# Fused LayerNorm, attention and mixture-of-experts on one core: the experts' code written out, their loop limits fetched early, and several pieces of work in a new order

## The chip, the cores and the metric

The kernel runs on one core of one Trainium2 chip. The metric is the device time of one execution in microseconds. A core has five engines with a sequencer each: TensorE (PE in the rows; its weight loads are PEld), VectorE (DVE), ScalarE (ACT), GpSimd (POOL) and SyncE (SP, which issues most DMAs). They work in parallel and meet only at semaphores.

## The reference

```python
xn = layernorm(x)                                   # x: 4 batches x 1024 rows x 256
q, k, v = xn @ Wq.T + bq, xn @ Wk.T + bk, xn @ Wv.T + bv
qk = einsum('bsd,btd->bst', q, k)
theta = 0.5 + 0.2 * sigmoid(qk) + 0.15 * tanh(qk) + 0.1 * relu(qk)
s = einsum('bst,btd->bsd', softmax(theta), v) @ Wo.T + bo
e = argmax(xn @ Wr + br)                            # one of 8 experts for each row
y = gelu(xn @ W1[e] + b1[e]) @ W2[e] + b2[e]        # hidden width 1024, exact gelu
out = x + s * silu(y)
```

## The kernel before

All products run on TensorE with operands split into a high and a low part. `product` (L812 to L815) makes three matmuls of one: high times high, high times low, low times high. So most operands are made in two steps: ScalarE or VectorE copies the high part (`high_...`), and VectorE subtracts it for the low part (`low_...`).

A tile is 128 rows of tokens; there are 32, eight to a batch. The order of the work is written out by hand on each engine, with semaphores in between. In order of time:

1. Batch 0. `scores(n)` makes the scores of tile n against its batch, `acts(n, h)` on ScalarE takes tanh and relu of each half, `thetas(n)` on VectorE mixes them and finds the greatest, `exps(n)` on ScalarE takes exp, `transposes(n)` on TensorE turns the result, `transposed_high` and `transposed_parts` split it, and `values(n)` multiplies it with v; `finish(n)` on VectorE scales the result. Between these, the other three batches are normalized (GpSimd, from `scales(3, ...)`), turned (`turn`, `keep_turned`), and their experts found (`route`, `take_turned`, `assign`). From the counts of tokens of each expert VectorE works out where each expert's units begin and end (`first_unit`, `last_unit`, `full_end`). The list of tokens sorted by expert is made with 32 small matmuls, `invert(t)`, eight of them behind the pieces of `values(5)`, 16 behind those of `values(6)`; they need `lanes` of VectorE and `token_at` of GpSimd.
2. The experts. A unit is 256 tokens of one expert, gathered by GpSimd. With the inputs of these runs there are 20, and the eight experts have 3, 1, 5, 1, 5, 1, 1 and 3 of them. TensorE does for each `hidden` (16 products, 48 matmuls), `turn_rows` of the next unit (4 transposes) and `expert_out` (8 products for each half of 128 tokens; where a unit holds at most 128, only one half). ScalarE does `gelus`, `row_high` and `gate`, VectorE `hidden_parts`, `row_low`, `biased` and `gated`. During the first unit of expert e the weights of e + 1 are split: `high_w1` and `high_w2` on ScalarE, `low_w1` and `low_w2` on VectorE, two pieces each. Experts 0 to 5 run in a loop over three pairs, with an inner loop over the units; 6 and 7 are written out. How far the inner loops run isn't known before the run: each engine reads `first_unit` and `full_end` into registers with `value_load` when it comes to an expert. Tiles 8 and 9 of batch 1 are scored between units of expert 7, and the rows of batch 2 are split by GpSimd (L492, L497).
3. Attention of batches 1 to 3, with the projections of the next batch (`job`) between.

An argument `head_slot` pads the code so that a loop's head stands at that slot of an instruction block.

## Time and profile before

| | |
|---|---|
| median of 3 runs | 550.07 us (549.77 to 550.94) |
| the profiled execution | 549.93 us, its span 548.1 us |
| TensorE busy in it | 526.6 us (96%) |
| VectorE, ScalarE, GpSimd busy | 413.5, 337.6, 206.3 us |
| the chain that ended last | TensorE 79%, VectorE 10%, ScalarE 5% |

TensorE sits idle for 21.5 us of the span. A matmul's end in the trace is modelled, so short pauses are seen in the distance from start to start rather than in the busy time. 1.8 us of the time lie outside the span.

### The profile page before, as it was taken

To read this page: it belongs to the slowest core of one execution; us is meant where nothing else is said; L and a number is where in the kernel's file an instruction comes from. 1 tells how busy PE (TensorE), PEld (TensorE's weight loads), DVE (VectorE), ACT (ScalarE), POOL (GpSimd) and SP (SyncE) were. 2 spreads that over 40 slices of the span, in tenths; PEclk is the share of its full clock that TensorE was granted. 3 is DMA by queue.
4 is the path that set the end of the run, shared out by engine and by line. 5 is a ranking of instruction groups with operands and counts; after the bars stand their busy time and mean duration, and the time that the engine had idled before them with its cause. 6 is when DMAs were issued, how large, how long until landed. Compare 5 with 4: busy or idle time off the path is not lost.

```text
span 548.1 us, 11163 instructions
## 1 busy us (share of the span) xinstructions
PE 526.6 (96%) x3891; PEld 496.4 (91%) x3892; DVE 413.5 (75%) x808; ACT 337.6 (62%) x607; POOL 206.3 (38%) x246
## 2 busy tenths in 40 slices
PE   7999999999999999999999989799999999999996
PEld 6888898998999999999999979798899899999995
DVE  6896688945588754787554897768899999777895
ACT  3587778536356733466433666278777877777881
POOL 2216338923112222122122214304467585333442
PEclk9999999999999999999999999999999999999999
DMA  8932920044315711146211411004132232111121
GB/s 285 333 153 107 337 78 1 1 139 160 125 59 150 245 45 50 46 148 226 85 38 52 130 50 39 19 21 155 59 108 95 88 115 88 59 42 46 59 67 49
DMA packets 40306, 56.88 MB, mean 104 GB/s; under 512 B 3607, under 2 KB 35358, under 8 KB 39726
## 3 DMA queue, kind: packets, MB, share of 16 engines
q1 hardware_dynamic: 35020, 45.62, 24.8%
q0 software_dynamic: 3488, 9.47, 6.0%
q10 hardware_dynamic: 1762, 1.32, 0.7%
q8 instruction: 20, 0.33, 0.2%
q14 instruction: 16, 0.13, 0.1%
HBM read 40.68 MB, written 17.56 MB: 106 GB/s over the span
## 4 chain that ended last, share of the span: by engine, by line
PE 79%; DVE 10%; ACT 5%; issue 4%; DMA 1%; DVEq 0%; ACTq 0%
PE ps L813 25%; PE ps L815 23%; PE ps L814 23%; PE ps L912 4%; PE ps L972 2%; PE ps L1085 1%; DVE stats L1220 1%; DVE theta L1278 1%; DVE theta L1274 1%; PE ps L962 1%; ACT theta L613 1%; ACT theta L603 1%; DMA xn_all<-in_L_attn_x_dram 1%; ACT tanh_s L604 1%; DVE u_lo L1255 0%
## 5 line engine op out<-in xcount | busy, mean ns | idle before, releaser
L712 ACT ACTIVATE hid<-ps,b_now 128x256 f32<-128x256 f32 x160 | 66.7, 471 | 42.3 <-PE ps L815 32.7
L813 PE MATMUL ps<-v_hi,pT_hi 128*128 128x258 f32 x256 | 76.2, 298 | 2.5 <-DVE pT_lo L1292 1.0
L814 PE MATMUL ps<-v_lo,pT_hi 128*128 128x258 f32 x256 | 72.5, 283 | 0.0
L815 PE MATMUL ps<-v_hi,pT_lo 128*128 128x258 f32 x256 | 72.3, 282 | 0.0
L1274 DVE SCALAR_TENSOR_TENSOR theta<-tanh_s,theta 128x512 f32<-128x512 f32 x64 | 49.1, 767 | 27.5 <-ACT tanh_s L604 26.8
L813 PE MATMUL ps<-rowT_h,w_hi_even 128*128 128x256 f32 x224 | 63.8, 285 | 1.1 <-issue 1.0
L815 PE MATMUL ps<-rowT_h,w_lo_even 128*128 128x256 f32 x224 | 63.5, 283 | 0.0
L814 PE MATMUL ps<-rowT_l,w_hi_even 128*128 128x256 f32 x224 | 63.4, 283 | 0.0
L483 POOL COPY unit_token<-sorted_token 128x2 int32 x19 | 4.6, 241 | 152.3 <-PE ps L1085 152.3
L613 ACT ACTIVATE theta<-theta,neg_max 128x512 f32<-128x512 f32 x64 | 42.9, 721 | 28.2 <-DVE neg_max L1278 27.9
L813 PE MATMUL ps<-w_hi_even,hidT_h 128*128 128x256 f32 x200 | 58.1, 291 | 0.2
L1546 DVE TENSOR_TENSOR hidT_l<-hid,hidT_h 128x512 fp32r<-128x512 f32 x80 | 55.4, 693 | 2.8
L815 PE MATMUL ps<-w_hi_even,hidT_l 128*128 128x256 f32 x200 | 56.6, 283 | 0.0
L814 PE MATMUL ps<-w_lo_even,hidT_h 128*128 128x256 f32 x200 | 56.6, 283 | 0.0
L720 ACT ACTIVATE g_sb<-y_sb 128x512 f32<-128x512 f32 x20 | 12.6, 632 | 70.1 <-DVE y_sb L1551 70.1
L603 ACT ACTIVATE theta<-ps,c_half 128x512 f32<-128x512 f32 x64 | 44.3, 692 | 18.6 <-PE ps L815 18.6
L813 PEld LDWEIGHTS ps<-v_hi,pT_hi 128*128 128x128 f32 x256 | 48.5, 189 | 3.7 <-issue 2.2
L813 PE MATMUL ps<-xnT_hi,u_hi 128*128 128x512 f32 x128 | 51.7, 404 | 0.0
L473 POOL DMA_INDIRECT row<-xn_rows,unit_token x38 | 43.6, 1147 | 20.7 <-POOL unit_token L483 14.9
L504 POOL DMA_INDIRECT g_tile<-sorted_g,slot_g x32 | 37.9, 1183 | 33.8 <-DMA sorted_g<-g_sb 28.4
L815 PE MATMUL ps<-xnT_hi,u_lo 128*128 128x512 f32 x128 | 50.2, 392 | 0.0
L814 PE MATMUL ps<-xnT_lo,u_hi 128*128 128x512 f32 x128 | 50.0, 391 | 0.0
(228 smaller groups left out, 1664.0 us busy)
## 6 DMA issues: line engine op xcount, KB each, us to landing
w_raw_odd<-in_L_ffn_W_dram SPq DMA_DIRECT2D x10, 1024.0 KB, 5.3
w_raw_even<-in_L_ffn_W_dram SPq DMA_DIRECT2D x6, 1024.0 KB, 6.6
sorted_g<-g_sb SPq DMA_DIRECT2D x20, 256.0 KB, 2.1
xn_rows<-xn_all SPq DMA_DIRECT2D x4, 1024.0 KB, 6.0
x_tile<-in_L_attn_x_dram SPq DMA_DIRECT2D x32, 128.0 KB, 2.2
out_dram<-g_tile SPq DMA_DIRECT2D x32, 128.0 KB, 1.7
xn_all<-in_L_attn_x_dram SPq DMA_DIRECT2D x3, 1024.0 KB, 12.1
kept_xT<-passing_xT SPq DMA_DIRECT2D x2, 1024.0 KB, 4.3
```

The costliest lines, as they stand in the source:

```text
L473: pool.indirect_dma_start(row[:, a, :], None, xn_rows, bass.IndirectOffsetOnAxis(ap=tokens[:, a:a + 1], axis=0)).then_inc(row_in, 16)
L504: pool.indirect_dma_start(g_tile[:, p % RING, :], None, sorted_g, bass.IndirectOffsetOnAxis(ap=slot_g[:, n:n + 1], axis=0)).then_inc(g_in[ ...
L603: nc.scalar.activation(theta[:, j % 2, cols], bank, ACT.Tanh, bias=c_half[:, n:n + 1], scale=0.5)
L613: nc.scalar.activation(part, part, ACT.Exp, bias=neg_max[:, j % 2, 1:2], scale=-1.0).then_inc(exp_done, 1)
L712: last = nc.scalar.activation(hid[:, j % 2, c * UNIT:(c + 1) * UNIT], ps[:, HID_BANK + j, c * UNIT:(c + 1) * UNIT], ACT.Gelu, bias=b1_now[ ...
L720: nc.scalar.activation(g_sb[:, :, :], y_sb[:, :, :], ACT.Tanh, scale=0.5).then_inc(y_tanh, 1)
L813: mm(dst, a_hi, b_hi, start=first, stop=False)
L814: mm(dst, a_hi, b_lo, start=False, stop=False)
L815: return mm(dst, a_lo, b_hi, start=False, stop=last)
L912: last = nc.tensor.transpose(ps[:, PT_BANK + h, i * P:(i + 1) * P], theta[:, n % 2, h * HALF + i * P:h * HALF + (i + 1) * P], ident[:, :])
L1274: v.scalar_tensor_tensor(part, tanh_s[:, cols], KT, part, ALU.mult, ALU.add).then_inc(mixed, 1)
L1546: v.tensor_tensor(hidT_l[:, now, :], gelu, hidT_h[:, now, :].bitcast(F32), ALU.subtract).then_inc(hidT_ready, 1)
```

## The change

It has six parts.

- The experts are written out, eight bodies on each engine in place of a loop over pairs. TensorE reads all limits with 16 `value_load` behind the pieces of `values(5)` and `values(6)`, and a seventeenth behind the projections of batch 1. ScalarE and VectorE read an expert's end during the expert before it. The wait for the b1 column and its copy move forward as well, into a double buffer.
- The first weights W1 are split by halves of the hidden columns in place of halves of the inner dimension. `hidden` begins once the first half is there and waits for the second in its middle. VectorE splits the first piece of the next W2 before `biased` of an expert's first unit, and the second before `gated` of its last.
- Batch 2's rows leave GpSimd: ScalarE makes the high part and VectorE the low one in the first unit of expert 7, and tile 8's `acts` and `thetas` go from that unit to the last but one.
- The seam to the attention: the first projection of batch 2 goes ahead of tile 9's scores, `weighted(8)` ahead of `transposes(9)`, and on VectorE `biased` of the last unit ahead of `thetas(9)`.
- Batch 0: `keep_turned` ahead of `acts(1)`, `take_turned(0)` ahead of the last `low_v`, `take_turned(1)` ahead of `finish(0)`, `finish(2)` ahead of the work on the counts.
- The scales of batches 1 and 2 are made ahead of tile 0's transposed parts on VectorE, and their square root ahead of `transposed_high(0)` on ScalarE.

The diff, cut to its core:

```diff
@@ lists of limits @@
-        first_unit, last_unit = sb("first_unit", [P, E + 1], I32), sb("last_unit", [P, 1], I32)
+        first_unit, last_unit = sb("first_unit", [P, E + 1], I32), sb("last_unit", [P, 2], I32)
@@ GpSimd: first weights, batch 2's rows @@
             def low_w1(e):
-                for i, piece in enumerate(halves(w1_hi[0])):
+                for i, cols in enumerate(HIDDEN_HALVES):
...
-            pool.wait_ge(kept_in, 16)
-            wait_apart(pool, y_done, before_last)
-            pieces = [slice(first, first + D) for first in range(0, S, D)]
-            for k in range(DC):
-                for cols in pieces:
-                    last = nc.gpsimd.tensor_copy(xnT_hi[place_of_batch(2)][:, k, cols], own_xT[:, k, cols])
-                last.then_inc(lnT_hi, 1)
-            for k in range(DC):
-                pool.wait_ge(lnT_hi, 4 + DC + k + 1)
-                for cols in pieces:
-                    last = nc.gpsimd.tensor_tensor(xnT_lo[place_of_batch(2)][:, k, cols], own_xT[:, k, cols],
-                                                   xnT_hi[place_of_batch(2)][:, k, cols].bitcast(F32), ALU.subtract)
-                last.then_inc(lnT_lo, 1)
@@ ScalarE: start @@
             exps(0)
-            acts(1, 0)
             for q in range(2, 4):
                 keep_turned(0, q)
-            acts(1, 1)
-            transposed_high(0)
+            for h in range(2):
+                acts(1, h)
             nc.scalar.activation(warm[:, 2:3], zeros[:, 0:1], ACT.Sqrt)
             square_root(3, slice(TPB, 3 * TPB))
+            transposed_high(0)
@@ ScalarE: experts @@
+            def units_of(e, u0, u1):
+
+                par, other = e % 2, 1 - e % 2
+                gelus(u0, par)
+                row_high(u0 + 1)
+                raw = raw_of(e + 1)
+                high_w1((w1_in[place_of(e + 1)], landed(e + 1)), other, raw[0], both)
+                high_w2((w2_in[place_of(e + 1)], landed(e + 1)), other, raw[1], both)
+                pick_b1(e + 1)
+                following = end_of(e + 1)
+                gate(u0)
                 with act.If(u0 + 1 < u1):
                     with act.Fori(u0 + 1, u1) as u:
-                        unit(u)
+                        unit(u, par)
+                return following
...
-            with act.Fori(0, E // 2 - 1) as pair:
-                for par in range(2):
-                    e = pair * 2 + par
-                    u0, u1 = units_of(e)
-                    pick_b1(e)
-                    first_unit_of(u0, 1 - par, pair + 2 - par)
-                    other_units(u0, u1)
+            for e in range(E - 1):
+                following = units_of(e, u0, u1)
+                u0, u1 = u1, following
...
+            with act.If(u7 < last_u):
+                gelus(u7, 1)
+                row_high(u7 + 1)
+                wait_apart(act, y_done, u7)
+                high_xT(2)
+                gate(u7)
...
+            with act.If(u7 + 1 < last_u):
...
+                gelus(before_last, 1)
+                row_high(last_u)
+                tile_8()
+                gate(before_last)
@@ TensorE @@
+                    if limited == "ends":
+                        end_of.append(pe.value_load(first_unit[0:1, i + 1:i + 2], min_val=1, max_val=MAX_UNITS))
+                    elif limited == "full":
+                        full_of.append(pe.value_load(full_end[0:1, i:i + 1], min_val=0, max_val=MAX_UNITS))
...
-            values(n - 2, inverted=[[i] for i in range(TPB)])
-            values(n - 1, inverted=[[TPB + 2 * i, TPB + 2 * i + 1] for i in range(TPB)])
+            values(n - 2, inverted=[[i] for i in range(TPB)], limited="ends")
+            values(n - 1, inverted=[[TPB + 2 * i, TPB + 2 * i + 1] for i in range(TPB)], limited="full")
...
+            def units(e, u0, u1):
+
+                par, split = e % 2, (e + 1) * 2
+                with nc.Fori(u0, u1, engines=bass.OrderedEngineSet([mybir.EngineType.PE]),
+                             head_slot={mybir.EngineType.PE: par * 128}) as u:
+                    hidden(u, par, split)
+                    turn_rows(u + 1)
+                    pe.wait_ge(w2_split, split)
+                    expert_out(u, par, full_of[e])
...
+            for e in range(E - 1):
+                pe.wait_ge(w1_split, e * 2 + 1)
+                units(e, end_of[e - 1] if e else 0, end_of[e])
...
+            pe.wait_ge(w1_split, E * 2 - 1)
+            with pe.If(u7 < last_u):
+                units(E - 1, u7, last_u)
+            hidden(last_u, 1, E * 2)
+            job(TPB + 1)
+            wait_apart(pe, gelu_done, last_u * 4 + 2)
+            scores(TPB + 1)
+            pe.wait_ge(w2_split, E * 2)
+            expert_out(last_u, 1, full_of[E - 1])
...
-                pe.wait_ge(pT_ready, n * 2)
                 if n == TPB + 1:
-                    job(n)
-                transposes(n)
...
+                    wait_apart(pe, y_biased, end_of[E - 1])
+                    weighted(n - 1)
+                    transposes(n)
+                else:
+                    pe.wait_ge(pT_ready, n * 2)
+                    transposes(n)
@@ VectorE @@
             thetas(1)
+            scales(3, TPB, 3 * TPB)
             transposed_parts(0)
-            scales(3, TPB, 3 * TPB)
-            for q in range(4):
+            for q in range(3):
                 low_v(0, q)
             take_turned(0)
+            low_v(0, 3)
...
+            take_turned(1)
             finish(0)
-            take_turned(1)
...
             transposed_parts(3)
+            finish(2)
             dve.wait_ge(ranks_done, 1)
...
-            finish(2)
             thetas(5)
...
+                for i, cols in enumerate(HIDDEN_HALVES):
+                    dve.wait_ge(w1_high, e * 2 + i + 3)
+                    v.tensor_tensor(w1_lo[other][:, :, cols], raw[:, :, cols],
+                                    w1_hi[other][:, :, cols].bitcast(F32), ALU.subtract).then_inc(w1_split, 1)
+                low_w2(e, other, 0)
+                following = end_of_units(e + 1)
+                dve.wait_ge(b2_in, e * 16 + 16)
                 biased(u, par)
+                return following
...
+            def end_of(u1, e, par):
+
+                low_w2(e, 1 - par, 1)
+                gated(u1 - 1)
...
+            with dve.If(u7 < last_u):
+                hidden_parts(u7)
+                row_low(u7 + 1)
+                low_xT(2)
+                biased(u7, 1)
+                gated(u7)
...
+                hidden_parts(before_last)
+                row_low(last_u)
+                thetas(TPB)
+                biased(before_last, 1)
+                gated(before_last)
...
+            biased(last_u, 1)
             thetas(TPB + 1)
-            biased(last_u, 1)
```

What TensorE is given in `values(5)`, before: after the transpose of the b1 rows come pieces of three matmuls, each with one small `invert` matmul behind it.

```order
L1059 MATMUL ps<-ident,b_rows 128x64
L813 MATMUL ps<-v_hi,pT_hi 128x258
L814 MATMUL ps<-v_lo,pT_hi 128x258
L815 MATMUL ps<-v_hi,pT_lo 128x258
L937 MATMUL ps<-token_at,at_lane 128x46
L813 MATMUL ps<-v_hi,pT_hi 128x258
```

The same place after the change (L819 to L821 are the lines of `product`, L948 is that of `invert`):

```order
L1070 MATMUL ps<-ident,b_rows 128x64
L819 MATMUL ps<-v_hi,pT_hi 128x258
L820 MATMUL ps<-v_lo,pT_hi 128x258
L821 MATMUL ps<-v_hi,pT_lo 128x258
L948 MATMUL ps<-token_at,at_lane 128x46
L939 TENSOR_LOAD first_unit
L939 ISA x2
L819 MATMUL ps<-v_hi,pT_hi 128x258
```

Behind each piece there is now a load of a limit and the two instructions that check its bounds, eight times here and eight times in `values(6)`, where the line is L941 and two `invert` stand in each piece.

GpSimd's end of the experts, before: the loop that gathers the units' tokens, batch 2's rows, and the gathers of the results.

```order
L483 COPY unit_token<-sorted_token 128x2
L473 DMA row<-xn_rows,unit_token 128x256 x2
L481 REGISTER_ALU
L481 COMPARE_AND_BRANCH
L492 CAST xnT_hi<-own_xT 128x256 x8
L497 TENSOR_TENSOR xnT_lo<-own_xT,xnT_hi 128x256 x8
```

VectorE in expert 7's first unit after the change: the last pieces of `hidden_parts`, `row_low`, batch 2's rows, `biased` and `gated`.

```order
L1550 CAST hidT_h<-hid 128x512
L1552 TENSOR_TENSOR hidT_l<-hid,hidT_h 128x512
L1540 REGISTER_ALU
L1541 TENSOR_TENSOR rowT_l<-ps,rowT_h 128x512
L1252 TENSOR_TENSOR xnT_lo<-own_xT,xnT_hi 128x1024 x2
L1556 REGISTER_ALU
L1557 TENSOR_TENSOR y_sb<-ps,b_all 128x512
L1563 SCALAR_TENSOR_TENSOR g_sb<-g_sb,y_sb 128x512
```

GpSimd's 16 instructions are gone, and two on VectorE (and two of ScalarE, ahead of its `gate`) stand in their place.

VectorE behind the last unit's `hidden_parts` after the change; before, `biased` (y_sb) stood behind the six rows of `thetas(9)` (theta, neg_max), right ahead of the two pT_lo:

```order
L1552 TENSOR_TENSOR hidT_l<-hid,hidT_h 128x512
L1556 REGISTER_ALU
L1557 TENSOR_TENSOR y_sb<-ps,b_all 128x512
L1278 SCALAR_TENSOR_TENSOR theta<-tanh_s,theta 128x512
L1282 ISA theta,neg_max<-theta,relu_s 128x512
L1282 ISA neg_max 128x1
L1278 SCALAR_TENSOR_TENSOR theta<-tanh_s,theta 128x512
L1282 ISA theta,neg_max<-theta,relu_s,neg_max 128x512
L1282 ISA neg_max 128x1
L1296 TENSOR_TENSOR pT_lo<-ps,pT_hi 128x512
L1298 TENSOR_TENSOR pT_lo<-ps,pT_hi 128x512
```

The wait of y_sb for the last unit's product now comes ahead of `thetas(9)`.

## Rows read from the trace of the kernel before

**Rows 1.** The page's first part: busy us, share, instructions.

```profile
PE 526.6 (96%) x3891; PEld 496.4 (91%) x3892; DVE 413.5 (75%) x808; ACT 337.6 (62%) x607; POOL 206.3 (38%) x246
```

**Rows 2.** TensorE's waits: what for, us in total, times, longest.

```profile
PE ps L813 <- DVE hidT_l L1546: 2.7, 1, 2.7
PE ps L813 <- DVE w_lo_odd L1568: 2.4, 1, 2.4
PE ps L813 <- issue: 2.4, 6, 0.8
PE ps L962 <- DVE c_half L1266: 1.4, 2, 1.0
...
PE ps L813 <- DVE half L1308: 0.9, 1, 0.9
```

**Rows 3.** TensorE's timeline at the experts: start, us, what, [idle before it <- releaser].

```profile
138.44 0.28 PE L813 MATMUL ps<-rowT_h,w_hi_even 128*128 128x256 f32 x1
...
144.20 0.60 PE L1085 MATMUL ps<-ident,row 128*128 128x128 f32 x4
...
150.40 0.28 PE L813 MATMUL ps<-rowT_h,w_hi_even 128*128 128x256 f32 x1
...
160.05 0.38 PE L813 MATMUL ps<-rowT_h,w_hi_odd 128*128 128x256 f32 x1 [0.42 <-issue]
...
320.27 0.36 PE L813 MATMUL ps<-w_hi_even,hidT_h 128*128 128x256 f32 x1
...
326.67 0.38 PE L813 MATMUL ps<-rowT_h,w_hi_odd 128*128 128x256 f32 x1 [2.38 <-DVE w_lo_odd L1568]
...
349.29 0.39 PE L813 MATMUL ps<-w_hi_odd,hidT_h 128*128 128x256 f32 x1 [2.73 <-DVE hidT_l L1546]
...
356.17 0.28 PE L813 MATMUL ps<-rowT_h,w_hi_odd 128*128 128x256 f32 x1
```

**Rows 4.** Windows: stretch, us, PE busy (matmuls), granted clock, DMA share, GB/s.

```profile
326.70:334.00 7.30, 7.30 (x48) 0.77 0.11 39
```

**Rows 5.** VectorE's timeline at expert 7.

```profile
323.78 2.35 DVE L1568 TENSOR_TENSOR w_lo_odd<-w_raw_odd,w_hi_odd 128x1024 fp32r<-128x1024 f32 x2
...
341.99 6.18 DVE L1557 SCALAR_TENSOR_TENSOR g_sb<-g_sb,y_sb 128x512 f32<-128x512 f32 x1 [0.90 <-ACT g_sb L720]
```

**Rows 6.** GpSimd's timeline at the same time.

```profile
342.06 5.55 POOL L497 TENSOR_TENSOR xnT_lo<-own_xT,xnT_hi 128x256 fp32r<-128x256 f32 x8
```

**Rows 7.** ScalarE's timeline: the high part of batch 1's rows.

```profile
99.82 2.02 ACT L583 ACTIVATE xnT_hi<-own_xT 128x1024 fp32r<-128x1024 f32 x2
```

**Rows 8.** Instructions of line L1196 on TensorE's sequencer: ns, first and last start.

```profile
L1196 PEldq TENSOR_LOAD <-first_unit x1: 316/316/316, 372.1 to 372.1; - x1
L1196 PEldq FUSED_REGOPS  x1: 156/156/156, 372.5 to 372.5; - x1
L1196 PEldq SEQ_ASSERT  x1: 18/18/18, 372.7 to 372.7; - x1
```

**Rows 9.** VectorE's timeline: its last piece for expert 0's last unit.

```profile
157.69 0.69 DVE L1546 TENSOR_TENSOR hidT_l<-hid,hidT_h 128x512 fp32r<-128x512 f32 x1
```

**Rows 10.** TensorE's sequencer right behind: the step of the loop, as rows 8.

```profile
L1140 PEldq ALU_OP  x1: 32/32/32, 158.5 to 158.5; - x1
```

**Rows 11.** TensorE's timeline: start of `values(5)`, end of `values(6)`.

```profile
97.71 0.39 PE L813 MATMUL ps<-v_hi,pT_hi 128*128 128x258 f32 x1
...
106.19 1.09 PE L912 MATMUL ps<-ident,theta 128*128 128x128 f32 x8
```

**Rows 12.** VectorE's timeline: the first piece of `lanes`.

```profile
95.17 1.22 DVE L1498 TENSOR_TENSOR at_lane<-lane,lane_id 128x1024 fp32r<-128x1024 f32 x1
```

**Rows 13.** TensorE's timeline: the first projection of batch 2; tile 10's transposes.

```profile
372.04 0.50 PE L813 MATMUL ps<-xnT_hi,M_hi 128*128 128x512 f32 x1 [0.69 <-DVE pT_lo L1294]
...
380.05 1.04 PE L912 MATMUL ps<-ident,theta 128*128 128x128 f32 x8
```

**Rows 14.** The page's third part: a DMA queue that brings instructions.

```profile
q8 instruction: 20, 0.33, 0.2%
```

More of the change, by code:

```diff
@@ L1 @@
-from contextlib import ExitStack
+from contextlib import ExitStack, nullcontext
 import concourse.bass as bass
@@ L586, in high_w1 @@
             def high_w1(landed, par, raw, pieces):
[L587 to L589 removed]
+                act.wait_ge(landed[0], landed[1] * 16)
+                for cols in HIDDEN_HALVES[pieces]:
+                    nc.scalar.activation(w1_hi[par][:, :, cols], raw[:, :, cols], ACT.Copy).then_inc(w1_high, 1)
             def high_w2(landed, par, raw, pieces):
[L592 removed]
+                act.wait_ge(landed[0], landed[1] * 16)
                 for piece in halves(raw)[pieces]:
@@ L775, in _, with tile_8 @@
+            u7 = u0
+            def tile_8():
+                act.wait_ge(c_ready, 5)
+                act.wait_ge(w1_split, 2 * E - 2)
+                act.wait_ge(w2_split, 2 * E - 2)
                 for h in range(2):
                     acts(TPB, h)
-                gate(u1)
-                with act.If(u1 + 1 < last_u):
-                    with act.Fori(u1 + 1, last_u) as u:
-                        unit(u)
-            with act.If(last_u < u1 + 1):
-                for h in range(2):
-                    acts(TPB, h)
@@ L787, in _ @@
+            with act.If(last_u < u7 + 2):
+                tile_8()
+            gelus(last_u, 1)
             nc.scalar.activation(warm[:, 3:4], zeros[:, 0:1], ACT.Exp)
@@ L1597, in _ @@
             row_low(0)
-            with dve.Fori(0, E // 2 - 1) as pair:
-                for par in range(2):
-                    e = pair * 2 + par
-                    u0, u1 = units_of(e)
-                    first_unit_of(u0, e, par)
-                    other_units(u0, u1, par)
-                    next_w2(u1, e, par)
-            u0, u1 = units_of(E - 2)
-            last_u = dve.value_load(last_unit[0:1, 0:1], min_val=E - 1, max_val=MAX_UNITS - 1)
-            first_unit_of(u0, E - 2, 0)
-            other_units(u0, u1, 0)
-            next_w2(u1, E - 2, 0)
-            dve.wait_ge(b2_in, 16 * E)
-            with dve.If(u1 < last_u):
-                hidden_parts(u1)
-                row_low(u1 + 1)
-                thetas(TPB)
-                biased(u1, 1)
-                gated(u1)
-                with dve.If(u1 + 1 < last_u):
-                    with dve.Fori(u1 + 1, last_u) as u:
+            u0, u1 = 0, end_of_units(0)
+            for e in range(E - 1):
+                if e == E - 2:
+                    last_u = dve.value_load(last_unit[0:1, 0:1], min_val=E - 1, max_val=MAX_UNITS - 1)
+                    before_last = dve.value_load(last_unit[0:1, 1:2], min_val=E - 2, max_val=MAX_UNITS - 2)
+                following = first_unit_of(u0, e, e % 2)
+                other_units(u0, u1, e % 2)
+                end_of(u1, e, e % 2)
+                u0, u1 = u1, following
+            u7 = u0
+            dve.wait_ge(b2_in, 16 * E)
+            with dve.If(u7 < last_u):
[4 more added lines that the diff above has]
+                gated(u7)
+            with dve.If(last_u < u7 + 1):
+                low_xT(2)
+            with dve.If(u7 + 1 < last_u):
+                with dve.If(u7 + 2 < last_u):
+                    with dve.Fori(u7 + 1, before_last) as u:
                         hidden_parts(u)
```

171 lines of the change are left out of this document (60 added, 111 removed).

## The prediction

> **What bounds the kernel now.** I read the busy times first: TensorE is busy for 526.6 of 548.1 us [rows 1], so a change can only take back its 21.5 us of idle time, or slow stretches inside the busy time, and anything that keeps TensorE waiting costs in full. The list of its waits [rows 2] names where the idle time is: 2.7 us for hidT_l, 2.4 for a low part of W1, 2.4 in six pauses of "issue" (no engine is waited for; TensorE's own sequencer is late), 1.4 for c_half in two pauses, 0.9 for half. Then TensorE's timeline gives the steady pace [rows 3]: `hidden` takes 144.20 - 138.44 = 5.76 us, a full unit 150.40 - 138.44 = 11.96. Where experts are long nothing is lost; the losses lie around the short experts 5 to 7.
>
> **Expert 7's start and end (the largest term).** Expert 6 is one unit with one half, 9.1 us for TensorE. VectorE needs more in it: eight copies and subtractions of 1.07 us a pair, two halves of W1 at 2.35 us for both [rows 5], W2 as much, and three shorter steps, 10.8 us together. So the order on VectorE decides. I count the losses from the half product of unit 16 to tile 10's transposes against the steady pace.
> - 320.27 to 326.67 is 6.40 us for 2.88 of work [rows 3]: 1.0 lost in waits between pieces, 2.5 in front of expert 7.
> - Then the granted clock is 0.77 on average over 7.3 us [rows 4], which is a while at 1.2 GHz in place of 2.4, right after this poor stretch; 7.3 us for 5.76 of work, 1.6 lost.
> - At 349.29 TensorE has waited 2.7 us (3.0 with the refill) for hidT_l, and takes 356.17 - 349.29 = 6.88 us for 5.84 of work [rows 3], 1.1 lost. The cause is one row: a g_sb of VectorE, 0.69 us elsewhere, takes 6.18 us from 341.99 [rows 5], just as GpSimd's subtraction of batch 2's rows runs from 342.06 for 5.55 us [rows 6]. VectorE sat behind GpSimd.
> - 0.9 at 372.04 for pT_lo [rows 13].
>
> Together 10.1 us. After the change I follow the chain by the same durations, in times of before. Without its loads ScalarE starts expert 6's units about a microsecond earlier, and VectorE's hidden_parts end near 321.9, row_low at 322.5, the first W1 half at 323.7. TensorE is done at 323.15 and may begin with that half: 0.7 lost, and too short a pause, I take it, to bring the lower clock. VectorE then still has the second W1 half, W2, biased and gated, so expert 7's first hidden_parts run from 328.5 to 332.7; TensorE wants the third piece at 331.4: 0.65 lost in two pauses. Batch 2's rows cost ScalarE 2.0 us [rows 7] and VectorE 2.35 (two subtractions of the shape of [rows 5]); VectorE does them until 335.7, and TensorE's product ends at 336.3, so they are hidden. Were VectorE over 2 us later, biased would be late, but nothing of TensorE hangs on it before the next hidden_parts. GpSimd's 5.55 us fall away, and with them 4.1. At the seam, biased waits for the last product and `thetas(9)` stand behind it: 0.6 + 2.9 + 0.6 us from 361.3 give the first pT_lo at 365.4, TensorE wants it at 364.8: 0.65. The projection moved forward fills 1.4 us of TensorE sooner than VectorE can use, so tile 9's parts come at 373.2 where TensorE wants them at 372.2: 1.05 more. Lost after: 3.05 us. **Gain 7.0 us**; if every new pause vanished 10.1, if each doubled 4.
>
> **The experts' edges.** 160.05 shows an idle 0.42 on issue [rows 3]; by start to start it is 0.58, since a steady matmul follows after 0.12. The four such edges lose 0.58, 0.36, 0.57 and 0.31, and the entry to expert 0 another 0.92. The sequencer loads limits there, with no more than a microsecond or two of matmuls given ahead. After the change no load stands there. A loop's step, branch and head remain, about 0.8 us behind the last matmul issued, as against 0.9 of lead after a half unit, so I leave 0.1 in all: **1.7 and 0.9 us gained**; nothing, if the jumps take as long.
>
> **Batch 0.** `take_turned(0)` comes 1.0 us earlier (its input by `keep_turned`, its place by one low_v), which is nearly the longer pause for c_half; `take_turned(1)` gives 0.2. `finish(2)` is waited for 0.9 us at 84.28 and now comes before 4 us of small steps; the steps come 0.7 later, and token_at is needed over 2 us after it is ready. 2.2 us so far, 1.5 of them also on VectorE, whose next thetas hang on ScalarE and on their own pace. The earlier scales only start GpSimd's normalizing, which has time.
>
> **The 16 loads.** The two pieced `values` take TensorE 8.5 us, 97.71 to 106.19 [rows 11], 0.47 and then 0.59 us a piece. A checked load holds the sequencer from 372.1 to past 372.7 [rows 8]: 0.32 + 0.16 + 0.02 us and three gaps of 0.06, 0.67. The matmuls go fast: VectorE's piece ends at about 158.35, and the loop's step behind the twelve instructions that waited for it is at 158.5 [rows 9, 10], so some 0.012 us each. A piece of values(5) so takes 0.77 us of the sequencer, one of values(6) 0.79, both more than TensorE needs. What is ahead at the start? The first `invert` waits for `lanes(0)`, done at 96.4 [rows 12], 94.9 after the 1.5 us above. From there 16 x 0.67 + 136 x 0.012 + 0.2 = 12.6 us, so tile 7's transposes start at 107.6, where before they did at 106.19. **1.4 us later, in place of 2.2 earlier**; the loads cost 3.6. Bounds: nothing, if the sequencer runs ahead unhindered (2.2 earlier); with 0.06 us for each matmul instruction too, the gap between control instructions, 6.5 more. I take the fast value, as its row is the same kind of instruction. The seventeenth load has 3.9 us of matmuls to cover it.
>
> **Sum.** + 1.4 - 0.9 - 1.7 - 7.0 = -8.2 against this execution's 549.93 us (span 548.1), so 541.7. The median of the runs is 550.07, 0.14 higher; I forecast 541.7. The last stages are the same code, and TensorE is bound there by itself.
>
> **Rivals.**
> 1. The loads are free, because the sequencer gets ahead where I have it held. Against it are the six issue pauses, which show that it is easily late; for it, that the pieces of values(6) are nearly long enough. 541.7 - 3.6 = 538.1. Chance 0.22.
> 2. The seam and the short experts lose more: VectorE and ScalarE carry over 10 us in a 9.1 us expert, and a pause like that at 324 brings 1.6 us of half clock again, here or in the thinned `values`, where TensorE would be busy for 60 to 75%. Two or three of these, 2 to 5 us: 543.5 to 546.5. Chance 0.25.
> 3. Slower: the eight bodies of TensorE are each entered by a jump to padded code that hasn't run, where the pair loop ran the same code three times. An instruction block takes 0.002 x 16 x 548 / 20 = 0.9 us of transfer [rows 14]; if each jump waits for a fetch from its issue, some 2 us more by a small transfer's landing, less the 1.3 us of lead, it costs 1.6 us, eight times 12.8: 554.5. It decides from 1.03 us a jump on. Against it: expert 6's code is also entered for the first time in the kernel before, and none of the issue pauses [rows 2] is there. Chance 0.05. The Trainium skill (Runtime: NRT & Kernel Launch, Instruction fetch mechanics) says that prefetch is sequential and that a taken branch out of the current window stalls for a fetch, but also that full unrolling is preferred. By its first sentence the time would be rival 3's; no row shows such a stall.
> 4. The edges change nothing and only the seam gains: 549.9 + 1.4 - 7.0 = 544.3. Chance 0.05.
>
> **How the numbers follow.** My forecast with its own range of 540 to 543.5 has 0.43. The range of 537.8 to 546 takes in rivals 1, 4 and most of 2, and leaves out rival 3, the far end of 2 and a gain above 12 us: 0.82. No change is within 0.2%, 1.1 us, which is what a measurement of this kernel can tell: it needs rival 3 in part or the loads at their upper bound. Faster 0.92, same 0.02, slower 0.06.
>
> **What would show it.** In `values(5)` TensorE pauses on issue some 0.2 to 0.3 us in each piece, and the TENSOR_LOADs stand 0.7 to 0.8 us apart; with rival 1 there is no pause. No issue pause of 0.4 at the experts' edges; with rival 3 pauses of over 1 us there, with new instruction packets. Expert 7 starts 0.7 us behind expert 6's last matmul, the clock stays at 2.4 GHz there, and no VectorE row takes 6 us. Around tile 10's scores two pauses for pT_lo. I would be wrong above all if the loads hold the sequencer differently in the middle of matmuls than at line L1196, or if one late chain at expert 7 brings the lower clock.

## The result, and the profile after

The kernel after takes 543.3 us (median of four runs, 541.4 to 546.0), the kernel before 549.9 beside it: ratio 0.9881, 95% interval 0.9836 to 0.9925. It is faster by 1.2%, 6.6 us, where 8.2 were forecast: inside the range, 1.6 us above the forecast. The profiled execution took 543.42 us (span 541.7).

The page after: busy time by engine, the queue that brings instructions, and below it TensorE's waits (us in total, times, longest), as [rows 1, 14, 2].

```profile
PE 524.9 (97%) x3891; PEld 495.8 (92%) x3891; DVE 410.8 (76%) x810; ACT 338.9 (63%) x608; POOL 197.7 (36%) x230
...
q8 instruction: 28, 0.46, 0.4%
```

```profile
PE ps L819 <- issue: 2.8, 5, 1.3
PE ps L819 <- DVE pT_lo L1296: 1.7, 2, 1.0
PE ps L973 <- DVE c_half L1270: 1.3, 2, 1.1
PE ps L819 <- DVE w_lo_odd L1574: 1.2, 1, 1.2
PE ps L918 <- DVE pT_lo L1298: 0.8, 1, 0.8
```

Three of the waits of before are gone (hidT_l, half, and one of 0.9 us for passing_xT, which [rows 2] leaves out), that for W1's low part is halved, and those for pT_lo have grown from 1.7 us in two pauses to 2.5 in three. But "issue" was meant to fall and has risen, with a longest pause of 1.3 us, and eight more instruction packets have come. TensorE's timeline after, at the places of [rows 3, 11, 13] (start, us, what, [idle before it <- releaser]):

```profile
95.50 0.39 PE L819 MATMUL ps<-v_hi,pT_hi 128*128 128x258 f32 x1
...
106.41 1.09 PE L918 MATMUL ps<-ident,theta 128*128 128x128 f32 x8
...
125.87 0.28 PE L819 MATMUL ps<-rowT_h,w_hi_even 128*128 128x256 f32 x1
...
172.45 0.38 PE L819 MATMUL ps<-rowT_h,w_hi_even 128*128 128x256 f32 x1 [1.26 <-issue]
...
241.83 0.38 PE L819 MATMUL ps<-rowT_h,w_hi_even 128*128 128x256 f32 x1 [0.28 <-issue]
...
314.42 0.38 PE L819 MATMUL ps<-rowT_h,w_hi_even 128*128 128x256 f32 x1 [0.62 <-issue]
...
324.94 0.38 PE L819 MATMUL ps<-rowT_h,w_hi_odd 128*128 128x256 f32 x1 [1.20 <-DVE w_lo_odd L1574]
...
366.20 0.36 PE L819 MATMUL ps<-v_hi,pT_hi 128*128 128x258 f32 x1 [0.71 <-DVE pT_lo L1296]
...
373.79 1.09 PE L918 MATMUL ps<-ident,theta 128*128 128x128 f32 x8 [0.82 <-DVE pT_lo L1298]
```

To read where the time went, I set the starts of the same instruction in both traces side by side:

| start of | before | after | difference | since the row above | forecast |
|---|---|---|---|---|---|
| `values(5)` | 97.71 | 95.50 | -2.21 | -2.2 | -2.2 |
| tile 7's transposes | 106.19 | 106.41 | +0.22 | +2.4 | +3.6 |
| expert 0 | 126.40 | 125.87 | -0.53 | -0.75 | -0.9 |
| expert 6 | 314.15 | 314.42 | +0.27 | +0.80 | -1.7 |
| tile 10's transposes | 380.05 | 373.79 | -6.26 | -6.5 | -7.0 |

The span is 6.4 us shorter. Four lines hold to 1.2 us or less, and in the fourth the sign is wrong: the six edges between experts 0 and 6 were to give back 1.7 us and cost 0.8 more. The three issue pauses stand where experts 2, 4 and 6 begin. The entries to experts 1, 3 and 5 have no pause, as forecast. TensorE's sequencer in front of the first pause, at the loop line L1136 (operation, count, duration in ns min/median/max, first and last start):

```profile
L1136 PEldq COMPARE_BRANCH  x2: 67/1500/2932, 169.0 to 169.4; - x2
```

One branch takes 2.93 us, and expert 2's first matmul stands right behind it; at the entry to expert 1 the same line takes 0.305 us. The other two take 2.12 and 2.45 us, less the sequencer's lead.

### The profile page after: what moved, and what is told of

Read it like the earlier page. It is cut to its first block, busy times and chain, and to the rows that moved or that the text cites. A ratio compares the mean times of both kernels' runs of the same rounds, so it can differ in the third digit from the quotient of the medians.

```text
span 541.7 us, 10966 instructions
## 1 busy us (share of the span) xinstructions
PE 524.9 (97%) x3891; PEld 495.8 (92%) x3891; DVE 410.8 (76%) x810; ACT 338.9 (63%) x608; POOL 197.7 (36%) x230
## 4 chain that ended last, share of the span: by engine, by line
PE 86%; DVE 7%; ACT 4%; issue 2%; DMA 1%; DVEq 0%; ACTq 0%
PE ps L819 27%; PE ps L821 25%; PE ps L820 25%; PE ps L918 5%; PE ps L1099 2%; DVE stats L1224 1%; PE ps L983 1%; PE ps L973 1%; DMA xn_all<-in_L_attn_x_dram 1%; DVE theta L1278 1%; DVE theta L1282 1%; ACT theta L608 1%; ACT theta L598 1%; ACT tanh_s L599 1%; DVE u_lo L1259 0%
## 5 line engine op out<-in xcount | busy, mean ns | idle before, releaser
L819 PE MATMUL ps<-v_hi,pT_hi 128*128 128x258 f32 x256 | 76.4, 298 | 2.6 <-DVE pT_lo L1296 1.7
L821 PE MATMUL ps<-v_hi,pT_lo 128*128 128x258 f32 x256 | 72.2, 282 | 0.0
L819 PE MATMUL ps<-rowT_h,w_hi_even 128*128 128x256 f32 x224 | 63.7, 284 | 2.2 <-issue 2.2
L1278 DVE SCALAR_TENSOR_TENSOR theta<-tanh_s,theta 128x512 f32<-128x512 f32 x64 | 48.0, 750 | 21.5 <-ACT tanh_s L599 20.9
L821 PE MATMUL ps<-rowT_h,w_lo_even 128*128 128x256 f32 x224 | 63.4, 283 | 0.0
L819 PE MATMUL ps<-w_hi_even,hidT_h 128*128 128x256 f32 x200 | 57.7, 289 | 0.0
L821 PE MATMUL ps<-w_hi_even,hidT_l 128*128 128x256 f32 x200 | 56.6, 283 | 0.0
L819 PEld LDWEIGHTS ps<-v_hi,pT_hi 128*128 128x128 f32 x256 | 48.3, 189 | 5.0 <-issue 3.7
L819 PE MATMUL ps<-xnT_hi,u_hi 128*128 128x512 f32 x128 | 51.7, 404 | 0.0
L1550 DVE CAST hidT_h<-hid 128x512 fp32r<-128x512 f32 x80 | 34.1, 427 | 22.9 <-ACT hid L707 22.4
L821 PE MATMUL ps<-xnT_hi,u_lo 128*128 128x512 f32 x128 | 50.2, 392 | 0.0
```

Source lines behind the costliest of these rows:

```text
L819: mm(dst, a_hi, b_hi, start=first, stop=False)
L821: return mm(dst, a_lo, b_hi, start=False, stop=last)
L1278: v.scalar_tensor_tensor(part, tanh_s[:, cols], KT, part, ALU.mult, ALU.add).then_inc(mixed, 1)
L1550: v.tensor_copy(hidT_h[:, now, :], gelu).then_inc(hidT_copied, 1)
```

## The experiments

"Kernel S" is that of the first experiment. Its runs differ by only 0.6 us from each other, the kernel after's by 4.6, so most later edits were made in kernel S. Each ratio is against the kernel before on the same chip. The median of the kernel before was 549.6 us beside e1 to e4, 550.0 beside e5 to e8 and 551.0 beside e9 to e12, so a difference of two medians from different groups is uncertain by about 1 us.

**e1_slot0 (kernel S).** Every body of TensorE's expert code begins at the start of an instruction block.

```
-                             head_slot={mybir.EngineType.PE: par * 128}) as u:
+                             head_slot={mybir.EngineType.PE: 0}) as u:
```

> The kernel after, with every expert body of TensorE headed at slot 0 of an instruction block, where odd experts were headed at slot 128 and their bodies lay over two blocks. Theory A: the three issue pauses behind odd experts (1.42, 0.45 and 0.79 us by start to start at 172, 242 and 314 us) come from a jump into a block whose fetch only begins at the jump, because the body before it ends in its second block. With every body in one block these go: no issue pause over 0.2 us between experts, jumps of about 0.3 us, some 2.4 us less, 540.9. Rival B: the fetch is late wherever the code is entered for the first time after a half unit, whatever the layout: the pauses stay, 543.3. Rival C: the layout only moves the stall to the other edges (behind experts 0, 2, 4, 6): 542 to 544.

Measured: 540.65 us, ratio 0.9819 (0.9790 to 0.9848). There is no issue pause between experts, and the loop line's slowest branch of the whole kernel is 0.33 us:

```profile
L1136 PEldq COMPARE_BRANCH  x27: 67/209/328, 124.4 to 344.4; - x27
```

Expert 6 starts 311.92 - 125.98 = 185.94 us after expert 0; before it was 187.75, in the kernel after 188.55. So the edges give 1.8 us here, which is the prediction's 1.7, and the stall cost 2.6. Rivals B and C are out. Theory A's cause is not yet shown by it.

**e2_slot128.** All bodies at slot 128, so all lie over two blocks (same line, `128` in place of `par * 128`).

> The kernel after, with every expert body of TensorE headed at slot 128, so that all eight lie over two blocks. Theory A (a body over two blocks leaves the next body's block unfetched): every one of the edges between experts stalls by 0.4 to 1.4 us, where three do now: four more at about 0.9 us, 546.9. Rival B (first entry costs whatever the layout is): as the kernel after, 543.3, with pauses at the same three edges.

Measured: 540.66 us, ratio 0.9820 (0.9790 to 0.9849), no pause between experts. I had expected 546.9. Theory A ("a body over two blocks leaves the next body's block unfetched") is wrong in this form. What differs from the kernel after is where the jump goes. A body has some 225 instructions (96 matmuls, as many weight loads, and the transposes, waits and branches). Here it ends in the first half of its second block, and the next begins at slot 128 of that same block. In the kernel after, an odd body ends there too, but the even one behind it begins in the block after: a third one, counted from the odd body's head. In e1_slot0 a body is one block, and the next is the second. So the three layouts agree with this: two blocks are held, and a jump to a third waits. The Trainium skill (Runtime: NRT & Kernel Launch, Instruction fetch mechanics) states just that, a window of two 16 KB blocks of 256 instructions each with sequential prefetch, and a stall for a jump out of it; the three runs agree, and the prediction, which quoted it, drew from it the wrong eight places.

The third block lies straight behind the one in which the odd body ends, just as in e1_slot0 the next body lies straight behind. The distance of the jump is thus not what differs, but the time that the fetch has. In e1_slot0 an instruction packet begins 1.0 to 1.7 us after each of the seven jumps between bodies, too late to be the block jumped to, so it brings the one behind that, a body ahead of the next jump. The packet ahead of the jump at 310.1 us came between 299 and 301 us and ended 9.4 us before it:

```profile
q8 instruction: 1, 0.02, 2.8%
```

In the kernel after, the sequencer is in the odd body's second block only for the end of that body.

**e10_w2_late.** Why does the stall vary, from 0.8 to 3.5 us, in kernels whose expert bodies on TensorE are the same (the kernel after, e3_loads_moved, e4_rows_gpsimd)? The kernel after, with W2's load of experts 3 and 5 issued an expert later; that of expert 7 stays as a control.

```
                 store_g(u0, u0 + 1)
+                if e in (1, 3):
+                    sp.wait_ge(w2_split, 2 * (e + 1))
+                    load_w2(e + 2)
...
-                if e + 3 < E:
+                if e + 3 < E and e not in (0, 2):
                     sp.wait_ge(w2_split, 2 * (e + 2))
```

> The kernel after (odd bodies headed at slot 128, so the pauses at 172, 242 and 314 us are in it), and in it the load of W2 for experts 3 and 5 is issued an expert later, behind the first store of experts 1 and 3 instead of ahead of it, so that no weights are on their way in the 7 us before the jumps out of experts 1 and 3; that of expert 7 stays. Theory A: the next block's fetch is asked for when TensorE's sequencer enters the second block of the odd body, some 5 us before the jump, and then waits behind the 1 MB of weights; without them it is there in time: no pause behind experts 1 and 3, the one behind expert 5 stays: 543.3 - 1.9 = 541.4. Rival B: the fetch is asked for at the jump itself: all three pauses stay, 543.3. Rival C: the W2 that comes later is late for VectorE's parts, and costs as much elsewhere.

Measured: 542.71 us (541.2 to 543.6), ratio 0.9847 (0.9818 to 0.9876). The DMA queues in the kernel after before and at the first slow jump (which begins at 169.4), windows of 162 to 168 and 169.5 to 171 us (packets, MB, share):

```profile
q1 hardware_dynamic: 1455, 1.44, 75.3%
```

```profile
q0 software_dynamic: 44, 0.13, 30.5%
q8 instruction: 1, 0.02, 3.8%
```

No instruction packet in the 6 us in which 1.44 MB of weights and rows pass; it comes only when they are through. In e10_w2_late, from 165 to 166.5 us:

```profile
q1 hardware_dynamic: 57, 0.05, 11.6%
q8 instruction: 1, 0.02, 5.2%
```

and its jump at 169.4, with below it the one behind expert 5, where the weights stayed in the way:

```profile
L1139 PEldq COMPARE_BRANCH  x2: 67/230/392, 169.2 to 169.4; - x2
```

```profile
L1139 PEldq COMPARE_BRANCH  x2: 70/618/1167, 309.7 to 309.9; - x2
```

The packet comes over 3 us ahead of the jump, and the jump takes 0.39 us; at the control it takes 1.17. So the fetch is asked for before the jump, and waits behind the weights. The ten slow jumps in the traces of the kernel after, e3, e4 and e10 say the same: each ends 1.36 to 1.50 us after the end of its packet, while for the two of 0.39 us the packet had ended 2.8 and 3.0 us before the jump's end; and at the six edges behind odd experts in e4 and e10 the packet begins within 0.1 us of the end of queue q1's last one (in the kernel after and e3 0 to 2.2 us behind it). Rival B is out, C too: TensorE's timeline is that of kernel S to 0.3 us up to 529 us. By the medians the run is worth 0.6 us, by the ratios to the kernel before 1.9, and the intervals of the two ratios overlap, so the time doesn't settle it; the trace does. The profiled execution (542.23 us) loses time in another place. From 532.5 us on it runs for a while at a lower granted clock, which kernel S's don't (windows: stretch, us, busy by engine, clock, DMA share, GB/s; first this run's, then kernel S's):

```profile
530.00:535.00 5.00, 4.04 (x24) 3.63 (x23) 1.29 (x2) 1.49 (x3) 1.45 (x2) 0.75 0.15 52
```

```profile
530.00:535.00 5.00, 4.04 (x32) 3.64 (x31) 1.36 (x3) 1.61 (x3) 1.45 (x2) 1.00 0.16 56
```

That costs 1.4 us, which is all that this execution's span has over kernel S's (540.5 for 539.1); e7_batch0_old's trace has such a stretch at the same place, the kernel after's and kernel S's have none there. It doesn't explain the two slowest executions (543.2 and 543.6 us), whose mean granted clock is 1.00 and for which there is no trace.

**e3_loads_moved.** The kernel after, with the sixteen loads of limits behind batch 1's eight projections.

```
                 u_product(1, q)
+                limits("ends", 2 * q)
+                limits("ends", 2 * q + 1)
...
+                v_product(1, q)
+                limits("full", 2 * q)
+                limits("full", 2 * q + 1)
```

> The kernel after, with the sixteen loads of the experts' limits taken out of values(5) and values(6) and placed by twos behind the four u_products and the four v_products of batch 1, whose 512-wide matmuls keep TensorE busy for over 2 us each. Theory A: in values(5) and values(6) the loads set the pace, as the two took 10.9 us there against 8.5 before; moved, tile 7's transposes come 2.4 us earlier, and expert 0 too if nothing else sets its start: 541.0. Rival B: what was held up is soaked up again before expert 0, as VectorE or ScalarE sets the pace of tile 8's scores and of expert 0's first rows: tile 7's transposes 2.4 us earlier, expert 0 under 0.5, 543. Rival C: the loads hold the sequencer in the new place too, 1.3 us a pair against some 2.8 us of matmuls: no gain.

Measured: 542.8 us (541.6 to 544.3), ratio 0.9855 (0.9825 to 0.9885). Tile 7's transposes start at 104.86 (106.41 after) and expert 0 at 124.74 (125.87). Moving the loads is thus worth 1.55 us here and not theory A's 2.4, as a new wait of 0.6 us for GpSimd's token_at has come in `values(6)`:

```profile
102.89 0.37 PE L952 MATMUL ps<-token_at,at_lane 128*128 128x46 f32 x2 [0.59 <-POOL token_at L473]
```

Expert 0 keeps 1.1 us of it, so rival C is out and B (under 0.5) too. They were lost again at the edges, where two of this run's three stalls are longer (3.48 and 3.12 us on the sequencer), and the first one is followed by a while at 1.2 GHz:

```profile
171.64 0.38 PE L819 MATMUL ps<-rowT_h,w_hi_even 128*128 128x256 f32 x1 [1.82 <-issue]
```

```profile
171.70:176.30 4.60, 4.60 (x26) 4.60 (x27) 1.70 (x3) 0.84 (x2) 0.00 (x0) 0.63 0.49 143
```

So in this layout a gain before the experts can't be read from the time at the end.

**e11_plain_full.** Kernel S, the loads of `full` without bounds.

```
-                    full_of.append(pe.value_load(full_end[0:1, i:i + 1], min_val=0, max_val=MAX_UNITS))
+                    full_of.append(pe.value_load(full_end[0:1, i:i + 1]))
```

> The kernel with all bodies headed at slot 0 (540.65), and in it the eight loads of `full` in values(6) go without their bounds, so that each is one TENSOR_LOAD without the FUSED_REGOPS and the SEQ_ASSERT behind it; those in values(5) stay. Theory A: the loads hold the sequencer one after the other, 0.66 us each with the bounds and some 0.35 without: a piece of values(6) is bound by TensorE's 0.59 us again, its eight pieces take 4.7 us in place of 5.7, those of values(5) still 0.66 to 0.81 each: tile 7's transposes 1.0 us earlier, 539.9. Rival B: it is the load's own way to memory and back that counts, or the wait of each load for the matmuls ahead of it, and the bounds are free: nothing changes, 540.65. Rival C: the time is soaked up before expert 0: tile 7's transposes 1 us earlier, the end the same.

Measured: 539.68 us (539.5 to 540.0), ratio 0.9791 (0.9771 to 0.9811). In the kernel after such a load is three instructions, here one:

```profile
L941 PEldq TENSOR_LOAD <-full_end x8: 297/301/309, 101.0 to 105.8; - x8
L941 PEldq FUSED_REGOPS  x8: 146/146/146, 101.3 to 106.1; - x8
L941 PEldq SEQ_ASSERT  x8: 18/18/18, 101.5 to 106.3; - x8
```

```profile
L941 PEldq TENSOR_LOAD <-full_end x8: 300/302/304, 101.0 to 103.9; - x8
```

Seven steps from the first to the last take 4.8 us with bounds, 0.69 each, and 2.9 without, 0.41. Tile 7's transposes come at 105.53 in place of 106.51, 0.98 us earlier, and the run is 0.97 us shorter by the medians. Theory A holds: the loads hold the sequencer one behind the other.

**e7_batch0_old.** Kernel S, batch 0's orders as before (the hunks of the diff at `keep_turned(0, q)`, `scales(3, ...)`, `take_turned(1)` and `finish(2)`, turned back).

> The kernel with all bodies headed at slot 0 (540.65), and in it batch 0's orders on VectorE and ScalarE as in the kernel before: take_turned, finish(0) and finish(2), keep_turned and the scales of batches 1 and 2 in their old places. Theory A (the prediction's 2.2 us): the pauses for c_half are 1.0 and 0.4 again, that for half 0.9, so values(5) starts 2.2 us later and all behind it too: 542.9. Rival B: the loads in values(5) and values(6) stand behind lanes(0) of GpSimd and not behind TensorE, so half of it is soaked up there: 541.7.

Measured: 542.52 us (542.2 to 543.5), ratio 0.9856 (0.9826 to 0.9885): 1.9 us more. `values(5)` starts at 97.97 for 95.50, 2.5 us later; tile 7's transposes 107.94 for 106.51; expert 0 127.40 for 125.98, 1.4 later. TensorE's timeline shows three pauses back:

```profile
37.65 0.65 PE L983 MATMUL ps<-small_w,passing_xT 128*128 128x48 f32 x4 [0.93 <-ACT passing_xT L553]
...
61.17 0.63 PE L973 MATMUL ps<-ident,xn_all 128*128 128x128 f32 x4 [0.37 <-DVE c_half L1270]
...
84.58 0.39 PE L819 MATMUL ps<-v_hi,pT_hi 128*128 128x258 f32 x1 [1.03 <-DVE half L1312]
```

Both theories hold a part: 2.5 us at `values(5)`, of which 1.0 is soaked up before tile 7's transposes, where the loads set the pace.

**e4_rows_gpsimd and e9_rows_gpsimd_slot0.** Batch 2's rows back on GpSimd, first in the kernel after, then in kernel S.

```
+            pool.wait_ge(kept_in, 16)
+            wait_apart(pool, y_done, before_last)
...
                 row_high(u7 + 1)
-                wait_apart(act, y_done, u7)
-                high_xT(2)
...
-                low_xT(2)
```

> The kernel after, with batch 2's rows back on GpSimd (copy and subtraction, after expert 6), and the two places on ScalarE and VectorE empty. Theory A: GpSimd's subtraction of 5.5 us holds a short VectorE operation of the seam (g_sb or biased) for 5 to 6 us again, and hidT_l of the last unit comes late: TensorE loses 3 to 4 us, 546.5 to 547.5. Rival B: the six us at 342 in the kernel before were a chance meeting; with expert 7 starting earlier GpSimd's work falls elsewhere, and VectorE and ScalarE are freed of 2.4 and 2.0 us: 543 or a little less, no VectorE row of 6 us.

> The kernel with all bodies headed at slot 0 (540.65, spread 0.6), and in it batch 2's rows back on GpSimd. It repeats e4_rows_gpsimd (548.01, 544.4 to 552.1) without the stalls at the edges. Theory A: GpSimd's subtraction of 5.5 us holds one short VectorE operation; whichever it meets, TensorE loses 2 to 9 us, and how much differs from execution to execution: a median of 543 to 546, a spread of several us. Rival B: the spread of that run came from the edges' stalls (0.3 to 3.2 us each), so here it is within 1 us, at 542 to 543 (the 1.9 us for hidT_l in its profile).

Measured: 548.01 us (544.4 to 552.1), ratio 0.9968 (0.9943 to 0.9993), and 544.17 us (544.1 to 544.8), ratio 0.9878 (0.9853 to 0.9902). The second against kernel S is 3.5 us by the medians, and its trace is 3.1 us later at the end (532.95 for 529.86). GpSimd's and VectorE's timelines of the second:

```profile
335.33 5.60 POOL L504 TENSOR_TENSOR xnT_lo<-own_xT,xnT_hi 128x256 fp32r<-128x256 f32 x8
```

```profile
336.08 5.40 DVE L1573 SCALAR_TENSOR_TENSOR g_sb<-g_sb,y_sb 128x512 f32<-128x512 f32 x1 [0.89 <-ACT g_sb L730]
```

It is [rows 5, 6] again: the same short VectorE row, 0.69 us elsewhere, as long as GpSimd's subtraction, and TensorE then waits 1.95 us for hidT_l at 342.60. The VectorE row had all that it waits for and had begun, so the engines don't meet only at semaphores, as I wrote at the start. Rival B of the first is out. Of the second, the level is theory A's (543 to 546), the spread rival B's: 0.8 us in four runs, where the first had 7.7 in twelve. So most of the first's spread seems to hang on the edges' stalls. (The first's profile is of its fastest execution, so what the slowest lost, and where, is not shown.)

**e5_both_halves.** Kernel S, TensorE waiting for both halves of W1 at an expert's start.

```
-                pe.wait_ge(w1_split, e * 2 + 1)
+                pe.wait_ge(w1_split, e * 2 + 2)
...
-            pe.wait_ge(w1_split, E * 2 - 1)
+            pe.wait_ge(w1_split, E * 2)
```

> The kernel with all bodies headed at slot 0 (540.65 us, spread 0.6), and in it TensorE waits at each expert's start for both halves of W1's low part, as in the kernel before, where it starts with the first half. Only expert 7 is short enough of time for it to matter. Theory A: VectorE's second half lands about 1.25 us behind the first, so expert 7 starts 1.25 us later, its pause is 2.5 us, and the clock falls to 1.2 GHz for a while as in the kernel before, 1.6 us more: 543.5. Rival B: the pause of 2.5 us alone, the clock stays: 541.9. Rival C: VectorE's hidden_parts are late anyway and TensorE loses the same further on: 540.7.

Measured: 543.27 us (541.5 to 543.6), ratio 0.9866 (0.9834 to 0.9897). The pause is 2.38 us again, as in [rows 3], and the clock behind it:

```profile
323.40:329.40 6.00, 6.00 (x38) 6.00 (x39) 4.26 (x8) 2.31 (x5) 0.00 (x0) 0.72 0.15 52
```

Expert 7 starts 0.96 us later than in kernel S, and its first unit takes 13.54 us for 12.04: 1.0 + 1.5 us. Theory A holds. A pause of 1.2 us there doesn't bring the lower clock, one of 2.4 does. The length alone doesn't decide it between them: in e4_rows_gpsimd the wait of 1.92 us for hidT_l at 342.2 is followed by a mean granted clock of 0.57 from 343 to 347 us, in e9_rows_gpsimd_slot0 that of 1.95 us by 1.00.

**e6_job_late.** Kernel S, the first projection of batch 2 behind the wait for y_biased.

```
             hidden(last_u, 1, E * 2)
-            job(TPB + 1)
...
                     wait_apart(pe, y_biased, end_of[E - 1])
+                    job(n)
                     weighted(n - 1)
```

> The kernel with all bodies headed at slot 0 (540.65), and in it the first projection of batch 2 (job of tile 9) stands behind the wait for y_biased again and not between the last hidden product and tile 9's scores. Theory A (the step of the prediction that the projection moved forward opens the pauses of 0.71 and 0.82 us for pT_lo): the first pause goes, as 1.7 us of projection lie over it, TensorE instead is held in expert_out or at gelu_done by at most as much: 539.9 to 540.7. Rival B: without it the last expert_out waits for VectorE's four hidden_parts (4.3 us of work against 2.9 us of scores), 1 us or more: 541.5.

Measured: 539.14 us (538.9 to 542.0), ratio 0.9805 (0.9772 to 0.9839): 1.5 us less, more than I expected. The first pT_lo pause of the seam is gone, the second is 0.37, and no new wait stands in expert_out. In kernel S the two cost 1.8 us by start to start, here 0.5.

**e8_best and e12_best_job_late.** Kernel S with the loads moved as in e3_loads_moved, and at the seam

```
-            biased(last_u, 1)
             thetas(TPB + 1)
+            biased(last_u, 1)
```

and then that with e6_job_late's edit as well.

> A version meant to beat both: all bodies headed at slot 0, the sixteen loads by twos behind batch 1's u_products and v_products, and at the seam thetas(9) ahead of the last biased, as in the kernel before. Theory A: the loads moved gave 1.25 us at expert 0's start, which the longer stalls at the edges took back; without those stalls it stays. At the seam VectorE sat idle for 5.0 us in front of biased, while the scores of tile 9 were there: thetas first end near 363 in place of 365.4 (times of after), pT_lo comes 1 us sooner, the pause of 0.71 goes and that of 0.82 shrinks: 1.0 to 1.5 us. Together 538.2. Rival B: with thetas first, biased (which TensorE waits for before the values of tile 8) is late by as much: the seam gains nothing, 539.4. Rival C: the loads gain nothing at expert 0 either: 540.6.

> e8_best (537.14) with the first projection of batch 2 behind the wait for y_biased, which alone gave 1.5 us over e1_slot0. Theory A: both edits take away the same two pauses for pT_lo at the seam, and e8_best has none left: no gain, 537.1. Rival B: e6_job_late gained where no pause is shown (its first transposes of the seam stand 1.7 us earlier, so VectorE's chain starts earlier), and the gains add up in part: 536.4. Rival C: with thetas first, biased comes later, and the projection behind it leaves TensorE waiting between the scores and biased: 538.

Measured: 537.14 us (536.9 to 538.5), ratio 0.9764 (0.9734 to 0.9795), and 537.31, ratio 0.9754 (0.9733 to 0.9775). e8_best is 6.2 us faster than the kernel after and 12.8 faster than before, by the medians. Its waits:

```profile
PE ps L819 <- DVE w_lo_odd L1580: 1.2, 1, 1.2
PE ps L819 <- DVE pT_lo L1302: 1.0, 1, 1.0
PE ps L819 <- issue: 0.6, 2, 0.3
PE ps L952 <- POOL token_at L473: 0.6, 1, 0.6
```

The 1.0 for pT_lo is at the kernel's very end; both pauses of the seam are gone, and from the start of the last `hidden` to tile 10's transposes it is 367.41 - 344.49 = 22.92 us, in kernel S 371.25 - 346.40 = 24.85. The loads give 1.4 at expert 0 (124.58 for 125.98). Together that is 3.3 us, more than theory A's 2.45, and rivals B and C are out. The projection's place adds nothing, as theory A of e12 said: two edits for the same pauses.

## Why the prediction was right or wrong, by its own steps

The forecast was 1.6 us off, and in part that is luck: the edges were 2.5 us worse than in its sum and the loads 1.2 us cheaper. With the loads at their forecast price the time would have been 544.5, outside my own range of 540 to 543.5.

- **Batch 0, 2.2 us.** Right in size (2.2 in the kernel after, 2.5 in e7_batch0_old), half wrong in place. I gave 1.0 of it to the longer pause for c_half. That pause stayed (1.1 us), and what went was one of 0.9 us for passing_xT at 37 us, by the same move of `keep_turned`, which the prediction didn't list.
- **The 16 loads, 3.6 us.** The mechanism was right: the TENSOR_LOADs stand 0.69 us apart, 0.65 to 0.80 a piece behind the first, and without bounds the stretch is TensorE's again (e11_plain_full). The size was 2.4. The term mis-sized is that of the matmuls: 16 x 0.68 = 10.9 us are the whole 10.9 from `values(5)` to tile 7's transposes, so the 136 x 0.012 don't add up behind the loads. Rival 1 (free loads) is out.
- **Expert 0's entry, 0.9.** Measured 0.75.
- **The edges, 1.7.** This step failed. Taking the loads away gives 1.8 us (e1_slot0), as worked out, but "a loop's step, branch and head remain, about 0.8 us" left out that three of the seven jumps go to a block that isn't there. Rival 3 named the mechanism, with 1.6 us a jump, and put it at all eight bodies. Measured are 2.1 to 2.9 us a jump in the profiled execution, less 1.5 to 1.7 of lead, at three edges. "Expert 6's code is also entered for the first time in the kernel before, and none of the issue pauses is there" was a bad argument: that code lay straight behind. The trace of before has an instruction packet at 161.0 us and the next at 315.7, 1.5 us into expert 6, so the code of expert 6 was there long before it was needed.
- **Expert 7's start and end, 7.0.** Measured 6.5. The pause in front is 1.2 and not 0.7: expert 6 began 0.27 us later for the edge's stall, VectorE's first W1 half (from 323.01) ends at 324.23, and then 0.7 us pass to the first matmul at 324.94. I had allowed almost nothing for those: expert 7's If and the loop's head stand behind the wait and not ahead of it (the head's branch is the row below, columns as above). There is no half clock, as forecast. The 0.65 us for hidT in expert 7 didn't come. Those at the seam did, nearly to the number: 0.71 for 0.65, 0.82 for 1.05. Of the 7.0 us, the rows off GpSimd are worth 3.1 to 3.5 (e9), starting on the first half 2.6 (e5); the projection moved forward and thetas behind biased cost 1.5 to 1.9, which e6_job_late and e8_best take back. That leaves some 2 us of the 6.5 that no run takes apart (the limits read ahead on ScalarE and VectorE, the earlier split of W2, `weighted(8)` moved forward).

```profile
L1136 PEldq COMPARE_BRANCH  x1: 295/295/295, 324.5 to 324.5; - x1
```

- **Rival 2** (more lost at the seam, half clock again) gave the right time, 543.5, for a reason that isn't its own.
- **What is left open.** The fetch waits behind the weights, and the jump to a third block waits for it: both shown. At which instruction the fetch is asked for is only bounded: before 165.7 us in e10_w2_late, over 3.6 us ahead of the jump. Nor does kernel S's rule, a packet soon after each new block is entered, hold in e2_slot128, where none comes between 129.6 and 155.7 us though each of expert 0's three units passes into the second block. The 1.4 us of lower clock at the kernel's end in some executions has no cause that a run here shows.

## What to carry to other kernels

Code that is written out in place of a loop has a layout: ask of every jump into a new block how long before it the sequencer entered the block that it leaves (a whole body, 9 us or more, was enough here; the second half of one was not with 1 MB of weights on the way), and what the DMA queues carry in that time. A register load with bounds is 0.69 us of the sequencer, and belongs behind matmuls that take longer than that. Where an engine sits idle for 5 us ahead of a step (VectorE before `biased`), look first for what could stand ahead of it.

## What the runs showed that I had not expected

- The same jump to a third block took the sequencer 0.8 to 3.5 us, by when its packet came behind what the DMA queues carried. The kernels with such jumps also differ more from run to run (4.6 us in the kernel after, 0.6 and 0.9 in e1_slot0 and e2_slot128), but with one trace of each it isn't shown that the jumps alone do it.
- An issue pause of 1.8 us at an expert's edge was followed by 4.6 us at a mean granted clock of 0.63 (e3_loads_moved), one of 1.26 us in the kernel after by none.
